# A fused decoder layer on one core: the SP queue's order and the interleaving of the other engines' steps are rewritten

## The chip, the core and the metric

The kernel runs on one core of one Trainium2 chip. The core has five engines that work side by side and meet only at semaphores: TensorE (PE in the profile: matrix products; PEld is its weight load), VectorE (DVE), ScalarE (ACT), GpSimd (POOL) and SyncE (SP, which here only issues DMA transfers). Each engine takes its instructions strictly in the order in which they are written. The metric is the device time of one execution in microseconds (us); of several runs the median counts.

## The reference

A decoder layer is applied to x of shape (32, 100, 256), 32 sequences of 100 tokens, with a context ctx of shape (32, 361, 256):

```
x = layernorm(x + self_attention(x))            # 16 local heads and 4 latent heads, mixed by a gate, then out_w
x = layernorm(x + cross_attention(x, ctx, ctx)) # 16 heads; q and k are normalised per head
x = layernorm(x + switch_ffn(x))                # 8 experts, 200 places each; a token without a place stays as it is
```

In the self-attention a gate mixes the two kinds of heads: `gate * local + (1 - gate) * remote`. In the cross-attention the scores are `layernorm(q Wq) @ layernorm(k Wk)` per head, then a softmax over the 361 context tokens.

## The kernel before

The sequences pass through one software pipeline. Each iteration `it` works on several sequences at once, one per stage: A (products of the self-attention) on sequence n+2, B (its gate, out projection, norm and the cross queries) and K (cross keys) on n+1, X (row maxima of the cross scores) and V (cross values) on n, Y (cross scores, exponentials, products with V) on n-1, T (norm, router, placing in the experts' buffers) on n-2. Steps of a stage are numbered: A1, A2, K12, K34, B1 to B7, T2 to T6, V5, V6, Y1, Y2. The loop has 36 iterations; in 28 of them every stage has work. Behind it the eight experts run one after the other; the change leaves them alone.

Each engine has a function `body(it)` that lists its steps in the order in which it does them; nothing else sets the order. What each engine has in it:

- **PE** (`body`, L1059): A1 and A2 are the products of xT with the weights; they wait for xT. `cross_maximum(it, n)` (L991), n = 0 to 15, forms the scores of one head for the row maxima. They lie in two buffers of PSUM (MX), so number n can start only when DVE has read number n-2. Number 0, called X0 here, also waits until the stacked keys (Kst) and queries (Qst) have landed. `self_maxima` (L853 to L865) does the same for the self-attention, `cross_scores` (L1009) and `self_scores` (L886, L891) form the scores for the exponentials. K12(it, t) (L825, L826 with cT) is half t of the key projection, K34 (L971) its mean square. B3 transposes `mixed`, B6 is the query projection, B7 (L960) its mean square from `sqq`, X1 (L997) transposes the maxima, Y1 and A6 are the products with the values, Y2 and A7 transpose their results back.
- The small products share two PSUM banks, MI0 and MI1. The list `MISC` gives the order of their use: its entries take the two banks in turn, and a step can start only when the step two entries before it has been read out (`enter`).
- **DVE**: copies A1 and A2 out into QK, takes the 16 `cross_max` (L1445) and two `self_max`, T3 (sum and statistics), `norm2`, B2, `gate_sum`, `gating` (it ends with `gated`), B4, `norm1`, `key_norm`, `key_low`, `route_to`, `place_in`, `queries`, Y2, A7.
- **ACT**: the exponentials `cross_exp` (L1207) and `self_exp` (L1197), copies out of PSUM (among them OxU, which empties Y1's bank), K12 and K34, `rstd`, `gate_exp`, `high_k`, `high_q`, B6 (qc, then sqq), B7.
- **POOL**: `pair_sums`, `self_lo`, `gate_local`, `gate_remote`, `mix` (it makes `mixed` from `gated`), `keep_x2`, `x1_bias`, `query_low`, `scatter`.
- **SP**: loads cT (L535), xT (L543) and xn (L551) for later sequences. QK, the keys and the queries are each written to DRAM (`bounce_...`, L564 and L586) and read back in another layout (`stack_...`, L574, L578, L597): the stack waits until the write has landed. `load_c` for n+2 waits until V6 of sequence n has read the old cT; `load_x` for n+3 until A2 of n+1 has read the old xT; `bounce_keys` waits for `key_low`, `bounce_queries` for `query_low`.

Of the kernel before, what the change touches and what calls it, by code (L numbers as in the profile page):

```python
# [59 lines left out]
MISC = ["A1", "A2", "T2", "K1", "B1", "T3", "B2", "K2", "K3", "T4", "B3", "K4", "B4", "A4", "T5", "V5", "T6",  # L60
        "B5", "B6", "X1", "B7", "Y1", "V6", "A6", "Y2", "A7"]
# [98 lines left out]
def decoder_kernel(nc, io):  # L160
    ctx = ExitStack()
    with ctx:
# [360 lines left out]
        def _(sp):  # L523
# [152 lines left out]
        def _(pool):  # L676
# [84 lines left out]
            def body(it):  # L761
# [32 lines left out]
        def _(pe):  # L794
# [266 lines left out]
            def body(it):  # L1061
# [8 lines left out]
                if x: cross_maximum(it, 2); cross_maximum(it, 3); cross_maximum(it, 4)  # L1070
                if b: B1(it)
                if t: T3(it)
                if y: cross_scores(it, 3)
                if x: cross_maximum(it, 5)
                if b: B2(it)
                if x: cross_maximum(it, 6)
                if y: cross_scores(it, 4)
                if k: K12(it, 1)
                if x: cross_maximum(it, 7); cross_maximum(it, 8); cross_maximum(it, 9)
                if k: K34(it, 0)  # L1080
# [9 lines left out]
                if y: cross_scores(it, 6)  # L1090
                if a: self_maxima(it, 1)
                if y: cross_scores(it, 7)
                if a: A4(it)
                if t: T5(it)
                if x: cross_maximum(it, 13)
                if v: V56(it, [0, 1])
                if t: T6(it)
                if x: cross_maximum(it, 14)
                if a: self_scores(it, 0)
# [676 lines left out]
```

## Time and profile before

| | |
|---|---|
| median of 3 runs | 1540.39 us (1537.62 to 1549.59) |
| profiled execution | 1558.85 us, of which the trace spans 1557.0 |
| PE busy | 1211.0 us, 78% of the span, 11098 matmuls |
| PEld, DVE, ACT, POOL busy | 881.9, 842.6, 673.5, 335.7 us |
| mean granted TensorE clock | 0.903 of full speed |
| DMA | 134.99 MB, 87 GB/s over the span |

PE is the busiest engine, and what matters is when it stands still in its main loop and for whom. A row of the timeline gives the start (us from the span's start), the duration, the engine, the line of the kernel, the operation, out<-in by the program's names, the shape, how many instructions the row merges and, in brackets, the idle time ahead of it and what ended it. SPq is SP's queue: its rows are DMA issues, not transfers. A share of busy time is an average over stages with different limits, so the argument goes by single iterations.

### The profile page before, as it was taken

The numbers are of one execution on the slowest core, as the hardware profiler recorded it, in microseconds if no ns is written. First come the engines' busy times: TensorE is split into PE (matmuls) and PEld (weight loads), VectorE is DVE, ScalarE is ACT, GpSimd is POOL, SyncE is SP. The second block draws the span as 40 slices with busy tenths as digits, with TensorE's granted clock in tenths as the row PEclk, the third lists the DMA queues.
The fourth block names the chain that finished last, engine by engine and source line by source line (L and its number), as shares of the span: only waits on it lengthen the run. The fifth ranks groups of instructions, "written<-read, shape, count | busy, mean of one in ns | idle before, by whom it ended". The sixth has DMA issues, their size and how long they took to land.

```text
span 1557.0 us, 33961 instructions
## 1 busy us (share of the span) xinstructions
PE 1211.0 (78%) x11098; PEld 881.9 (57%) x11098; DVE 842.6 (54%) x2482; ACT 673.5 (43%) x1611; POOL 335.7 (22%) x485
## 2 busy tenths in 40 slices
PE   3577777888778888888887888788878887675885
PEld 2355555555555555666555566565555565454774
DVE  4234456566665656565556665666566655433432
ACT  0123445444454445444545454555455545432110
POOL 2111112122222222222222222222212222100111
PEclk9667989899999989889999999999999989866998
DMA  4233332233333333333333333334333333106542
GB/s 152 50 78 70 83 85 62 64 86 86 75 84 84 84 84 84 84 84 82 85 78 86 78 77 81 87 74 91 76 84 84 84 83 76 45 10 211 194 148 72
DMA packets 187012, 134.99 MB, mean 87 GB/s; under 512 B 95798, under 2 KB 182762, under 8 KB 186734
## 3 DMA queue, kind: packets, MB, share of 16 engines
q1 hardware_dynamic: 181778, 127.50, 34.3%
q0 software_dynamic: 3200, 6.61, 1.4%
q8 instruction: 29, 0.48, 0.1%
q10 hardware_dynamic: 1984, 0.23, 0.1%
q14 instruction: 21, 0.17, 0.0%
HBM read 91.06 MB, written 43.00 MB: 86 GB/s over the span
## 4 chain that ended last, share of the span: by engine, by line
PE 32%; issue 15%; DVE 14%; DMA 9%; POOL 5%; ACT 4%; SPq 3%; DVEq 1%; POOLq 0%; ACTq 0%
PE MI L825 7%; PE MI L826 6%; DMA xT<-in_xT 5%; PE MI L1022 4%; PE MX L1138 4%; DVE negmax_x L1445 3%; DVE negmax_s L1438 2%; DVE Khl L1520 2%; PE ST L825 2%; PE ST L826 1%; DMA self_stack<-self_halves 1%; ACT QKhl L1214 1%; PE MX L853 1%; PE MI L971 1%; SPq L535 1%
## 5 line engine op out<-in xcount | busy, mean ns | idle before, releaser
L1445 DVE TENSOR_REDUCE negmax_x<-MX 100x1 bf16<-100x361 f32 x512 | 261.6, 529 | 108.9 <-PE MX L991 107.9
L1207 ACT ACTIVATE wide<-ST 128x800 f32<-128x800 f32 (+1 forms) x256 | 169.9, 665 | 345.8 <-PE ST L1009 345.0
L991 PE MATMUL MX<-stacked,Qst 96*128 96x361 f16 x512 | 154.8, 331 | 119.0 <-DVE negmax_x L1445 67.1
L991 PEld LDWEIGHTS MX<-stacked,Qst 96*128 96x128 f16 x512 | 53.0, 106 | 201.0 <-DVE negmax_x L1445 133.1
L825 PE MATMUL MI<-xT,weights 128*128 128x100 f32 (+1 forms) x320 | 78.0, 333 | 49.2 <-DMA xT<-in_xT 48.3
L719 POOL TENSOR_TENSOR QKhl<-QK,QKhl 128x900 f16<-128x900 f32 x32 | 60.5, 1890 | 256.2 <-ACT QKhl L1214 256.2
L1009 PE MATMUL ST<-Qst,stacked 112*128 112x200 f16 x768 | 112.1, 257 | 0.3 <-ACT wide L1207 0.3
L1416 DVE TENSOR_SCALAR QK<-MI,small,parity_s 128x100 f32<-128x100 f32 x128 | 42.6, 374 | 103.4 <-PE MI L826 99.4
L734 POOL TENSOR_TENSOR x_all<-x,bpv 100x256 f32 (+1 forms) x32 | 23.2, 725 | 342.5 <-DVE x L1496 342.5
L825 PEld LDWEIGHTS MI<-xT,weights 128*128 128x128 f32 (+1 forms) x320 | 56.7, 224 | 69.7 <-DMA xT<-in_xT 40.0
L1009 PEld LDWEIGHTS ST<-Qst,stacked 112*128 112x128 f16 x768 | 70.7, 102 | 29.2 <-issue 10.1
L725 POOL TENSOR_TENSOR Qhl<-Qx,Qhl 128x400 f16<-128x400 f32 x32 | 30.2, 945 | 235.6 <-ACT Qhl L1279 235.6
L1022 PE MATMUL MI<-wide,Vx 128*32 128x100 f32 (+1 forms) x3072 | 78.3, 260 | 0.0
L1022 PEld LDWEIGHTS MI<-wide,Vx 128*32 128x32 f32 (+1 forms) x3072 | 70.9, 115 | 7.5 <-issue 7.4
L826 PE MATMUL MI<-xT,weights 128*128 128x100 f32 (+1 forms) x320 | 74.2, 322 | 0.0
L853 PE MATMUL MX<-mask_q,identb 100*128 100x400 bf16 (+1 forms) x128 | 46.3, 453 | 30.0 <-DMA self_stack<-self_halves 26.2
L1438 DVE TENSOR_REDUCE negmax_s<-MX 100x8 bf16<-100x800 f32 x64 | 63.0, 984 | 4.2 <-PE MX L859 4.2
L1197 ACT ACTIVATE Ps<-ST 100x800 f32<-100x800 f32 x64 | 53.4, 834 | 24.7 <-PE ST L891 24.7
L825 PE MATMUL MI<-weights,cT 128*128 128x256 f32 (+1 forms) x192 | 63.7, 414 | 0.5 <-issue 0.5
L1502 DVE TENSOR_TENSOR qn<-qc,rsq 128x200 f32<-128x200 f32 x32 | 11.8, 368 | 92.6 <-ACT rsq L1266 92.6
L971 PE MATMUL MI<-early,small 128*128 128x361 f32 x128 | 60.1, 555 | 1.1
L826 PEld LDWEIGHTS MI<-xT,weights 128*128 128x128 f32 (+1 forms) x320 | 59.4, 229 | 0.0
(259 smaller groups left out, 2889.7 us busy)
## 6 DMA issues: line engine op xcount, KB each, us to landing
stacked<-key_halves SPq DMA_DIRECT2D x96, 180.5 KB, 4.7
self_halves<-QKhl SPq DMA_DIRECT2D x32, 450.0 KB, 2.9
cT<-in_cT SPq DMA_DIRECT2D x32, 361.0 KB, 3.7
key_halves<-Khl SPq DMA_DIRECT2D x32, 361.0 KB, 2.8
self_stack<-self_halves SPq DMA_DIRECT2D x64, 150.0 KB, 3.9
Qst<-query_halves SPq DMA_DIRECT2D x96, 100.0 KB, 4.3
early<-in_w SPq DMA_DIRECT2D x8, 1024.0 KB
self_stack<-self_halves SPq DMA_DIRECT2D x32, 225.0 KB, 3.7
```

Of the source, the lines that this page charges most:

```text
L719: pool.tensor_tensor(QKhl[:, LOW], QK[:].rearrange("p t n -> p (t n)"), QKhl[:, HIGH], ALU.subtract).then_inc(a_lo, 1)
L825: pe.matmul(out, lhs(0), rhs(0), start=True, stop=False)
L826: return pe.matmul(out, lhs(1), rhs(1), start=False, stop=True)
L853: pe.matmul(MX[:, i, 0:n], identb[0:S], mask_q[:, 0:n], start=True, stop=True)
L971: pe.matmul(ps[:, 0:M], average[:], sqk[:, t], start=True, stop=True).then_inc(filled[step], 1)
L991: pe.matmul(MX[:, n % 2, 0:M], Qst[p][0:96, n * S:n * S + 128], Kst[p][0:96, n // 2 * M:(n // 2 + 1) * M], start=True, stop=True).then_inc ...
L1009: mm = pe.matmul(ST[:, first + i, c:c + 2 * S], Kst[p][:, k:k + 128], Qst[p][:, 2 * pair * S:2 * (pair + 1) * S], start=True, stop=True)
L1022: mm = pe.matmul(ps[VW * j:VW * (j + 1), g * S:(g + 1) * S], Vx[p][0:n, kt, 4 * g + j], Px[0:n, c:c + S], start=(kt == 0), stop=(kt == 2))
L1138: mm = pe.matmul(MX[0:S, s, 0:D], hT[:, m, s * S:(s + 1) * S], W2[p][:, m], start=(m == 0), stop=(m == 7))
L1207: act.activation(cross_part(Px, u), ST[0:n, first:first + 2, 0:width], ACT.Exp).then_inc(st_exp, 1)
L1438: dve.tensor_reduce(out[:, 2 * g:2 * g + 2], MX[0:S, :, 0:400].rearrange("p i (u k) -> p i u k", k=S), X, ALU.max, negate=True).then_inc(m ...
L1445: dve.tensor_reduce(negmax_x[:, n:n + 1], MX[0:S, n % 2, 0:M], X, ALU.max, negate=True).then_inc(max_read, 1)
```

## The change

Only the order of steps changes; no instruction is added or taken away apart from the register moves that go with waits. SP's `body` is written anew:

```diff
             def body(it):
+                if it.n + 3 < B:
+                    load_x(Seq(it.n + 3, it.j))
+                if it.n + 2 < B:
+                    load_n(Seq(it.n + 2, it.j))
                 if it.has("A"):
                     bounce_self(it)
                     stack_self(it)
                 if it.has("K"):
                     bounce_keys(it)
-                if it.n + 2 < B:
-                    load_c(Seq(it.n + 2, it.j))
-                if it.n + 3 < B:
-                    load_x(Seq(it.n + 3, it.j))
+                    stack_keys(it)
                 if it.has("B"):
                     bounce_queries(it)
                 if it.n + 2 < B:
-                    load_n(Seq(it.n + 2, it.j))
-                if it.has("K"):
-                    stack_keys(it)
+                    load_c(Seq(it.n + 2, it.j))
                 if it.has("B"):
                     stack_queries(it)
```

So xT and xn are loaded at the head of the round, the keys' stack stands directly behind the keys' write, and cT is loaded between the queries' write and their stack. On POOL `mix` moves ahead of `keep_x2`, and `x1_bias` behind `query_low`:

```diff
-                if b: gate_local(Bs, it); gate_remote(Bs, it)
+                if b: gate_local(Bs, it); gate_remote(Bs, it); mix(Bs)
                 if t: keep_x2(T)
-                if b: mix(Bs); x1_bias(Bs); query_low(it)
+                if b: query_low(it); x1_bias(Bs)
                 if t: scatter(T)
```

On PE, DVE and ACT many steps change places, and `MISC` follows PE's new order. The parts of which the prediction speaks, PE's first, then ACT's, then DVE's:

```diff
+                if k: K12(it, 0)
                 if x: cross_maximum(it, 0); cross_maximum(it, 1)
-                if k: K12(it, 0)
...
+                if k: K34(it, 0); K12(it, 1)
                 if x: cross_maximum(it, 10)
+                if b: B3(it)
                 if y: cross_scores(it, 5)
                 if x: cross_maximum(it, 11)
+                if y: cross_scores(it, 6)
                 if t: T4(it)
                 if x: cross_maximum(it, 12)
-                if b: B3(it)
...
                 if b: B6(it)
-                if x: cross_maximum(it, 15); X1(it)
                 if a: self_scores(it, 2)
+                if x: X1(it)
                 if b: B7(it)
...
+                if a: self_exp(it, 1)
                 if b: B6(it)
                 if x: X1(it)
-                if a: self_exp(it, 1)
-                if b: B7(it)
+                if a: self_exp(it, 2)
+                if b: B7(it); high_q(it)
                 if y: copy_out("Y1", it, OxU[:], lambda ps: ps[:, 0:4 * S], (filled["Y2"], it.of("Y").done(back=1)))
-                if a: self_exp(it, 2)
-                if b: high_q(it)
...
                 if x: cross_max(it, 5)
+                if b: B2(it)
+                if x: cross_max(it, 6); cross_max(it, 7)
                 if t: T3(it)
-                if b: B2(it)
-                if x: cross_max(it, 6)
```

The new text is one line shorter by line 793, so PE's lines are one less after the change (L991 is L990).

PE, from the last products of A2 (MI<-rkvh,pairsum) to the first maxima of the cross scores (L991) before:

```order
L826 MATMUL MI<-rkvh,pairsum 50x64
L1009 MATMUL ST<-Qst,stacked 128x200 x4
L935 MATMUL MI<-small,Ox 128x100 x2
L1009 MATMUL ST<-Qst,stacked 128x200 x2
L991 MATMUL MX<-stacked,Qst 128x361 x2
L825 MATMUL MI<-cT,WkC 128x361
L826 MATMUL MI<-cT,WkC 128x361
```

The same place after the change:

```order
L825 MATMUL MI<-rkvh,pairsum 50x64
L1008 MATMUL ST<-Qst,stacked 128x200 x4
L934 MATMUL MI<-small,Ox 128x100 x2
L1008 MATMUL ST<-Qst,stacked 128x200 x2
L824 MATMUL MI<-cT,WkC 128x361
L825 MATMUL MI<-cT,WkC 128x361
L990 MATMUL MX<-stacked,Qst 128x361 x2
```

K12(it, 0) (MI<-cT,WkC) moved from behind the first two maxima to ahead of them.

PE, from K34(it, 0) (L971, MI<-early,small) to `self_maxima(it, 0)` (L853) before; MI<-small,mixed is B3 and MI<-small,x2w is T4:

```order
L971 MATMUL MI<-early,small 128x361
L991 MATMUL MX<-stacked,Qst 128x361
L1009 MATMUL ST<-Qst,stacked 128x200 x2
L991 MATMUL MX<-stacked,Qst 128x361
L935 MATMUL MI<-small,x2w 128x100 x2
L991 MATMUL MX<-stacked,Qst 128x361
L935 MATMUL MI<-small,mixed 128x100 x2
L971 MATMUL MI<-early,small 128x361
L853 MATMUL MX<-mask_q,identb 128x500 x2
```

The same place after the change:

```order
L970 MATMUL MI<-early,small 128x361
L824 MATMUL MI<-cT,WkC 128x361
L825 MATMUL MI<-cT,WkC 128x361
L990 MATMUL MX<-stacked,Qst 128x361
L934 MATMUL MI<-small,mixed 128x100 x2
L1008 MATMUL ST<-Qst,stacked 128x200 x2
L990 MATMUL MX<-stacked,Qst 128x361
L1008 MATMUL ST<-Qst,stacked 128x200 x4
L934 MATMUL MI<-small,x2w 128x100 x2
L990 MATMUL MX<-stacked,Qst 128x361
L970 MATMUL MI<-early,small 128x361
L852 MATMUL MX<-mask_q,identb 128x500 x2
```

B3 moved from behind the last of the thirteen maxima to directly behind the eleventh.

ACT, from the copy of x1T (B5) to the end of the iteration before; Ps and Pl are `self_exp`, qc and sqq B6, lnq and rsq B7, OxU the copy of Y1, Qhl `high_q`:

```order
L1163 ACTIVATE x1T<-MI 128x200
L1273 ACTIVATE Khl<-early,small 128x361
L1197 ACTIVATE Ps<-ST 100x800
L1254 ACTIVATE qc<-MI,bqC 128x100 x2
L1258 ACTIVATE sqq<-MI,bqC 128x100 x2
L1231 ACTIVATE turned_x<-MI 16x100
L1233 DMA Qst<-turned_x 1x16x100
L1197 ACTIVATE Ps<-ST 100x800
L1264 ACTIVATE lnq<-MI,eps 128x200
L1266 ACTIVATE rsq<-lnq 128x200
L1163 ACTIVATE OxU<-MI 128x400
L1197 ACTIVATE Pl<-ST 50x400
```

The same place after the change:

```order
L1197 ACTIVATE Ps<-ST 100x800
L1254 ACTIVATE qc<-MI,bqC 128x100 x2
L1258 ACTIVATE sqq<-MI,bqC 128x100 x2
L1231 ACTIVATE turned_x<-MI 16x100
L1233 DMA Qst<-turned_x 1x16x100
L1197 ACTIVATE Pl<-ST 50x400
L1264 ACTIVATE lnq<-MI,eps 128x200
L1266 ACTIVATE rsq<-lnq 128x200
L1279 ACTIVATE Qhl<-Qx 128x400
L1163 ACTIVATE OxU<-MI 128x400
```

The second `self_exp` now stands ahead of B6, the third ahead of B7, and the copy to OxU behind `high_q`.

## Rows read from the trace of the kernel before

**Rows 1.** Windows: stretch, its us, each engine's busy us (instructions), granted clock, DMA
```profile
436.95:1279.80 842.85, 689.08 (x6909) 493.33 (x6910) 510.85 (x1491) 421.91 (x1008) 204.85 (x295) 0.95 0.37 82
...
801.91:840.75 38.84, 31.04 (x329) 22.21 (x330) 24.34 (x71) 20.06 (x48) 9.75 (x14) 1.00 0.37 83
840.75:880.79 40.04, 32.16 (x329) 23.07 (x329) 24.34 (x71) 20.17 (x48) 9.75 (x14) 0.96 0.37 81
```

**Rows 2.** Waits of PE: for what, total us, times, longest us
```profile
PE MI L825 <- DMA xT<-in_xT: 48.3, 29, 4.3
PE MX L991 <- DMA Qst<-query_halves: 45.9, 21, 7.0
```

**Rows 3.** Timeline of SP's queue, one iteration: issue's start us, duration us, transfer
```profile
831.76 0.36 SPq L586 DMA_DIRECT2D key_halves<-Khl  x1
836.77 0.62 SPq L535 DMA_DIRECT2D cT<-in_cT  x1
837.68 0.59 SPq L543 DMA_DIRECT2D xT<-in_xT  x1
838.51 0.41 SPq L586 DMA_DIRECT2D query_halves<-Qhl  x1
...
841.91 1.87 SPq L597 DMA_DIRECT2D Qst<-query_halves  x3
```

**Rows 4.** Timeline of PE, the same iteration and the next one's start
```profile
808.44 0.47 PE L991 MATMUL MX<-stacked,Qst 96*128 96x361 f16 x2 [1.90 <-DMA Qst<-query_halves]
808.78 0.85 PE L825 MATMUL MI<-cT,WkC 128*128 128x361 f32 x2
...
810.07 0.51 PE L1009 MATMUL ST<-Qst,stacked 112*128 112x200 f16 x4
...
819.82 0.34 PE L935 MATMUL MI<-small,mixed 100*128 100x100 f32 x2
...
821.19 0.59 PE L853 MATMUL MX<-mask_q,identb 100*128 100x500 bf16 x2
...
832.20 0.22 PE L997 MATMUL MI<-identb,negmax_x 100*128 100x100 bf16 x1 [0.97 <-DVE negmax_x L1445]
...
832.74 0.53 PE L960 MATMUL MI<-sqq,small 128*128 128x200 f32 x2
...
836.49 0.89 PE L905 MATMUL MI<-Ps,Vs 100*32 100x100 f32 x32
...
840.75 0.47 PE L825 MATMUL MI<-xT,weights 128*128 128x100 f32 x2 [1.39 <-DMA xT<-in_xT]
...
847.60 0.47 PE L991 MATMUL MX<-stacked,Qst 96*128 96x361 f16 x2 [2.22 <-DMA Qst<-query_halves]
```

**Rows 5.** Timeline of DVE, the same iteration
```profile
806.83 0.25 DVE L1429 TENSOR_SCALAR QK<-MI,small 64x50 f32<-64x50 f32 x1
808.88 0.98 DVE L1445 TENSOR_REDUCE negmax_x<-MX 100x1 bf16<-100x361 f32 x2 [1.80 <-PE MX L991]
810.77 1.49 DVE L1445 TENSOR_REDUCE negmax_x<-MX 100x1 bf16<-100x361 f32 x3 [0.92 <-PE MX L991]
...
818.28 0.42 DVE L1477 TENSOR_TENSOR gated<-differ,gate 100x256 f32<-100x256 f32 x1
```

**Rows 6.** Timeline of POOL, the same iteration
```profile
818.87 0.72 POOL L730 TENSOR_TENSOR mixed<-gated,rem 100x256 f32<-100x256 f32 x1 [1.02 <-DVE gated L1477]
...
837.01 0.95 POOL L725 TENSOR_TENSOR Qhl<-Qx,Qhl 128x400 f16<-128x400 f32 x1 [7.22 <-ACT Qhl L1279]
```

**Rows 7.** Timeline of ACT, the same iteration
```profile
831.58 0.58 ACT L1258 ACTIVATE sqq<-MI,bqC 128x100 f32<-128x100 f32 x2
...
833.47 0.84 ACT L1197 ACTIVATE Ps<-ST 100x800 f32<-100x800 f32 x1 [0.69 <-PE ST L891]
...
835.55 0.51 ACT L1163 ACTIVATE OxU<-MI 128x400 f32<-128x400 f32 x1 [0.51 <-PE MI L1022]
...
836.33 0.53 ACT L1279 ACTIVATE Qhl<-Qx 128x400 f16<-128x400 f32 x1
```

More of the change, by code:

```diff
@@ L1089, in body @@
                 if b: B4(it)
-                if y: cross_scores(it, 6)
+                if y: cross_scores(it, 7)
                 if a: self_maxima(it, 1)
-                if y: cross_scores(it, 7)
+                if t: T5(it)
                 if a: A4(it)
-                if t: T5(it)
                 if x: cross_maximum(it, 13)
                 if v: V56(it, [0, 1])
+                if x: cross_maximum(it, 14)
+                if b: B5(it)
+                if a: self_scores(it, 0)
+                if x: cross_maximum(it, 15)
                 if t: T6(it)
-                if x: cross_maximum(it, 14)
-                if a: self_scores(it, 0)
-                if b: B5(it)
                 if a: self_scores(it, 1)
                 if b: B6(it)
-                if x: cross_maximum(it, 15); X1(it)
                 if a: self_scores(it, 2)
+                if x: X1(it)
                 if b: B7(it)
@@ L1291, in body @@
                 a, k, b, x, y, t, v = (it.has(stage) for stage in "AKBXYTV")
-                if y: cross_exp(it, 0)
+                if y: cross_exp(it, 0); cross_exp(it, 1)
+                if a: self_hi(it)
                 if t: copy_out("T2", it, OxT[:], halves)
-                if y: cross_exp(it, 1)
-                if a: self_hi(it)
                 if k: K12(it, 0)
+                if b: copy_out("B1", it, latT[:], lambda ps: ps[0:64, 0:S])
                 if y: cross_exp(it, 2)
-                if b: copy_out("B1", it, latT[:], lambda ps: ps[0:64, 0:S])
+                if t: rstd(it.of("T"), rs2, ln2, mv2, t_ln, t_rs)
                 if y: cross_exp(it, 3)
-                if t: rstd(it.of("T"), rs2, ln2, mv2, t_ln, t_rs)
+                if b: gate_exp(it)
                 if y: cross_exp(it, 4)
-                if k: K12(it, 1)
-                if b: gate_exp(it)
-                if k: K34(it, 0)
-                if y: cross_exp(it, 5)
+                if k: K34(it, 0); K12(it, 1)
+                if b: copy_out("B3", it, mixT[:], halves)
+                if y: cross_exp(it, 5); cross_exp(it, 6)
                 if t: copy_out("T4", it, x2T[:], halves)
-                if b: copy_out("B3", it, mixT[:], halves)
-                if k: high_k(it, 0); K34(it, 1)
-                if y: cross_exp(it, 6)
+                if k: K34(it, 1)
+                if y: cross_exp(it, 7)
                 if a: A4(it)
+                if b: rstd(it.of("B"), rs1, ln1, mv1, b_ln, b_rs)
+                if k: high_k(it, 0)
                 if t: router_exp(it)
-                if y: cross_exp(it, 7)
-                if b: rstd(it.of("B"), rs1, ln1, mv1, b_ln, b_rs)
                 if v: values(it, [0, 1])
                 if b: copy_out("B5", it, x1T[:], halves)
+                if a: self_exp(it, 0)
                 if k: high_k(it, 1)
-                if a: self_exp(it, 0)
+                if a: self_exp(it, 1)
                 if b: B6(it)
                 if x: X1(it)
-                if a: self_exp(it, 1)
-                if b: B7(it)
+                if a: self_exp(it, 2)
+                if b: B7(it); high_q(it)
                 if y: copy_out("Y1", it, OxU[:], lambda ps: ps[:, 0:4 * S], (filled["Y2"], it.of("Y").done(back=1)))
-                if a: self_exp(it, 2)
-                if b: high_q(it)
                 if v: values(it, [2])
@@ L1611, in body @@
                 if a: self_max(it, 1)
+                if t: route_to(it)
+                if b: norm1(it)
+                if x: cross_max(it, 13); cross_max(it, 14)
                 if k: key_norm(it, 1)
[L1613 to L1616 removed]
+                if x: cross_max(it, 15)
+                if k: key_low(it, 0); key_low(it, 1)
                 if t: place_in(it)
[L1618 to L1620 removed]
                 if b: queries(it)
```

33 lines of the change are left out of this document (12 added, 21 removed).

## The prediction

> **What bounds the kernel now.** The main loop comes first. Between 436.95 and 1279.80 us, 21 iterations take 842.85 us, 40.14 each; one that keeps the full TensorE clock takes 38.84, with PE busy for 31.04 of it [rows 1]. 24.34 of DVE, 20.06 of ACT and 9.75 of POOL lie inside the same stretch [rows 1], so PE is the engine that the others must not make wait. Next, who it waits for. Over the whole run it waits 48.3 us at A1, the first product of an iteration, until xT has landed, 29 times (1.67 each), and 45.9 us at X0 (`cross_maximum(it, 0)`) until Qst has landed, 21 times [rows 2].
>
> The reason for the first stands in SP's queue, which works strictly in order. It writes the keys at 831.76 and then stands at `load_c` until V6, the last reader of the old cT, is done; cT goes out at 836.77, xT behind it at 837.68, the queries' write at 838.51, and the queries' stack only at 841.91 [rows 3]. A1 then starts at 840.75 after 1.39 of waiting and X0 at 847.60 after 2.22 [rows 4].
>
> **The path of one iteration** closes over three legs [rows 1, 4]:
> - leg I, A1 to X0: 801.91 to 808.44, 6.53;
> - leg II, X0 to the first matmul of `self_maxima(it, 0)` (L853): 808.44 to 821.19, 12.75;
> - leg III, from there to the next A1: 821.19 to 840.75, 19.56.
>
> The three make 38.84. I work out what the change does to each.
>
> **Leg I: 6.5, no gain.** K12(0) now stands ahead of X0. It needs the MI bank that A2 filled, and that is free when the last QK write ends: 806.83 + 0.25 = 807.08 [rows 5], 5.2 after A1. K12(0) itself takes 808.78 to 810.07, 1.29 [rows 4]. So X0 comes 5.2 + 1.3 = 6.5 after A1. Qst could in principle let X0 start earlier, but PE is not there earlier. If the bank were free at once, up to 1.3 less; I take 0.
>
> **Is Qst there by then?** `query_low` ends at 837.01 + 0.95 = 837.96 [rows 6]. SP is then free, because `stack_keys` has its own place behind the keys' write: that write took until 834.9 at most (831.76 plus about 3.4, what the queries' write of 838.51 to 841.91 took [rows 3]), and with three issues taking 1.87 as for Qst [rows 3] the keys' stack is out near 836.8. The queries' write goes at 838.0 and not 838.51. To its stack it is 3.40, from the stack to X0 another 5.69 (841.91 to 847.60) [rows 3, 4]: X0 could start at 847.1, or 25.9 after `self_maxima`, with B7 as late as now. B7 comes 0.2 earlier (leg III): 25.7. Today three keys' transfers lie just ahead of the queries' stack and after the change one cT does, so I take 0.5 off as an estimate: 25.2. PE would be at X0 after the new leg III (18.6) plus 6.5, at 25.1. X0 waits 0.1 to 0.6; I take 0.15.
>
> Here a rule speaks against the change. The Trainium skill, "DMA: Bandwidth & Descriptors", section "Queues, rings and completion order", says that SP owns one row of rings and that each DMA engine takes descriptors in ring order. By it the cT that now goes out between the queries' write and their stack stands ahead of the stack, and nothing may be taken off: X0 waits 0.6 and the sum below turns from -0.25 to +0.2 an iteration. The row of the queries' write (3.40 with cT and xT ahead of it) neither shows nor excludes that; it is the third rival.
>
> **Leg II: 12.75 to 13.35, +0.6.** DVE is the pace here, and what counts are the holes in its row of maxima.
> - The hole of 0.92 that K12(0) makes between the second and third maximum [rows 5] goes: -0.92.
> - B3, the transpose of `mixed`, stood behind the last of these maxima; now it stands right behind the eleventh, on an engine that works in order, ahead of the twelfth. `mixed` ends at 818.87 + 0.72 = 819.59 [rows 6], 0.89 after its input `gated` (818.28 + 0.42 = 818.70 [rows 5]). Then come B3's 0.34 [rows 4] and 0.44 from a maximum's matmul to its reduce (808.44 to 808.88 [rows 4, 5]): 1.67 without a new maximum, less the 0.5 that the eleventh takes (0.98 for two [rows 5]): +1.15. PE meanwhile stands idle for longer, since the eleventh matmul needs only the ninth reduce: about 2.5.
> - DVE now takes B2's sum right behind the sixth maximum, while PE has to do the seventh first: a hole between 0 and the 0.92 that K12(0) makes; I take +0.4.
>
> Sum: +0.6, with ends of -0.9 (nothing lost) and +1.2 (both holes at their largest). T3's place and Y6's only exchange neighbours; the self-attention's stack needs nothing earlier than now, because PE gets to it no earlier.
>
> **Leg III: 19.56 to 18.55, -1.0.**
> - xT is loaded at the start of the SP round, an iteration ahead: -1.39 [rows 4].
> - X1's wait of 0.97 for the last maximum [rows 4] goes, because that maximum stands two steps earlier. But B7 follows X1, and it needs `sqq` from ACT. That ends now at 831.58 + 0.58 = 832.16, 0.58 before B7 (832.74) [rows 4, 7]. ACT's new order puts `self_exp(it, 1)`, 0.84 [rows 7], and one `high_k` ahead of it and takes the last `cross_exp` away. Of the 0.97 at most all and at least nothing is left; I take -0.2.
> - A6 needs the bank that Y1 filled, so it needs ACT's copy to OxU. That copy ends at 836.06 now, 0.43 before A6 (836.49) [rows 4, 7]. In the new order it stands behind `high_q`, which starts at 836.33 and waits for DVE [rows 7]: 836.33 + 0.43 to the next ACT step + 0.51 = 837.3, 0.8 after A6. With B7 0.2 earlier: +0.6 (ends 0 and 0.8).
>
> POOL's moved steps (`mix` ahead of `keep_x2`, `query_low` ahead of `x1_bias`) cost nothing: 29 us of each iteration it is idle [rows 1], and the next reader of `x1_bias` is an iteration away. Without that cover each would cost its 0.72 or so [rows 6].
>
> **The sum** is 0 + 0.6 - 1.0 + 0.15 = -0.25 an iteration, times the 28 in which every stage runs: -7. The waits for xT above 1.39 (48.3 - 29 x 1.39 = 8 us [rows 2, 4]) I count by half: -4. Together -11 on the profiled execution's own 1558.85 (span 1557.0 and 1.85 around it): 1548. That execution was 18.5 above the median of the runs, 1540.39, so in runs it is 1529; I say **1528**.
>
> **The clock** is the term I cannot sum. An iteration with the granted clock at 0.96 takes 40.04 against 38.84 at 1.00 [rows 1]: 1.20 for a short fall to the lower of the two levels (1.2 and 2.4 GHz). The mean iteration loses 1.30 that way [rows 1]. The change closes the idle time at the iteration's start and opens a longer one at B3. In the forecast these cancel.
>
> **Rivals.**
> 1. *The gain is large.* Falls of the clock go with the waits at A1 and X0. All iterations at full clock and 38.84 - 0.25 = 38.6: 28 x (38.6 - 40.14) = -43, and 4 for the long waits: 1540 - 47 = 1493. For it: A1's and X0's waits, 3.6 together in one iteration [rows 4], are the largest pair. Against it: B3's. Chance 0.23.
> 2. *Slower: B3 costs clock.* An idle PE of 2.5 in one piece exceeds each of today's (2.22 at X0 [rows 4]). If each iteration falls once more, it is 1.20 - 0.25 = +0.95, 28 x 0.95 = +27: 1567. It decides from a fall more in two of three iterations (0.67 x 1.20 - 0.25 = 0.55, 28 x 0.55 = 15.4, one per cent). The Trainium skill, "TensorE: Matmul & The Clock Gate", Part 1, says that the lower clock is the default and activity lifts it; that is this rival's mechanism. The rows bear it out in part only: the iteration from 801.91 has all of today's waits and keeps 1.00 [rows 1]. Chance 0.22.
> 3. *The change buys nothing, since Qst is the bound.* X0 waits for as long as A1 gained: +0.2 an iteration and long waits that only move: 28 x 0.2 = +6, 1546; with leg III's gain whole, 1535. I put it at 1542. Chance 0.13.
>
> **Chances and range.** The forecast has 0.42 and its own range of 1512 to 1545 (legs II and III at half of their ends). A measurement of this kernel can tell about one per cent, 15.4 us, from no change. Faster by more than that (below 1525): rival 1 and 0.17 of the forecast, 0.40. Within one per cent: 0.24 of the forecast and 0.12 of rival 3, 0.36. Slower: rival 2 and 0.02 left, 0.24. The range leaves out a tenth on each side: from rival 1's 1493 to 1562, five below rival 2.
>
> **What would show it.** Right: no wait for xT at A1; K12(0) ahead of X0 waiting for QK; a PE idle of 2 to 3 before B3 for `mixed`; X1 without a wait, B7 waiting for `sqq`, A6 for OxU; an iteration of 38.4 to 38.7 at full clock. Wrong: leg II at 12 or less (B3's wait hidden), X0 waiting over 1 for Qst (rival 3), the granted clock in the loop above 0.98 (rival 1) or below 0.93 (rival 2, today 0.95 [rows 1]).

## The result and the profile after

The changed kernel takes **1501.26 us** (median of 4 runs, 1497.61 to 1504.92); the kernel before took 1544.61 beside it (4 runs). The ratio is 0.972, with a 95% interval of 0.967 to 0.978: faster by 2.8%. The prediction was 1528, with a range of 1493 to 1562. The time lies in the range but below the forecast's own 1512 to 1545: the sign was right, and the gain was 43 where the sum had 11. That it lies in the range is in part luck: the range's lower end, 1493, was set for rival 1, whose mechanism did not occur.

Windows of the changed kernel: iterations five to ten of the loop, the 21 behind them that answer to the first of [rows 1], and one at full clock (stretch, its us, busy us and instructions of PE, PEld, DVE, ACT and POOL, granted clock, DMA):

```profile
178.80:410.60 231.80, 196.44 (x1977) 140.56 (x1975) 143.38 (x426) 116.79 (x288) 57.80 (x83) 0.95 0.36 86
410.60:1231.00 820.40, 686.32 (x6910) 493.09 (x6909) 503.87 (x1491) 409.63 (x1008) 204.66 (x295) 0.95 0.36 84
488.00:525.96 37.96, 30.95 (x331) 22.43 (x330) 24.03 (x71) 19.44 (x48) 9.81 (x15) 1.00 0.38 88
```

Iterations five to ten of the kernel before:

```profile
185.80:436.90 251.10, 201.89 (x1974) 144.81 (x1974) 146.20 (x426) 121.11 (x288) 58.52 (x84) 0.92 0.35 79
```

The span fell from 1557.0 to 1503.1, by 53.9; the profiled execution before was a long one, so this is more than the 43 between the medians. Of the 53.9, 19.3 lie in these six iterations (251.10 to 231.80), 10 in the four ahead of them (162.1 to 152.2, from A1 to A1 in the timeline), 22.5 in the 21 steady ones (842.85 to 820.40, which is 40.14 to 39.07 each) and 2 in the rest. An iteration at full clock went from 38.84 [rows 1] to 37.96. The mean clock of the steady stretch is 0.95 before and after.

Waits of PE after (for what, total us, times, longest us), to set against [rows 2]:

```profile
PE MI L934 <- POOL mixed L729: 55.9, 30, 3.6
...
PE MI L959 <- ACT sqq L1258: 22.2, 31, 1.0
...
PE MI L824 <- DVE QK L1426: 16.7, 28, 0.6
...
PE MI L904 <- ACT OxU L1163: 10.5, 28, 0.4
```

The two waits of [rows 2], for xT and for Qst, are gone (Qst keeps 6.9 us in two waits at the start), and four waits that the prediction named stand in their place. PE's timeline of the iteration from 488.00 shows their places:

```profile
493.22 0.88 PE L824 MATMUL MI<-cT,WkC 128*128 128x361 f32 x2 [0.60 <-DVE QK L1426]
...
494.54 0.47 PE L990 MATMUL MX<-stacked,Qst 96*128 96x361 f16 x2
...
505.68 0.36 PE L934 MATMUL MI<-small,mixed 100*128 100x100 f32 x2 [2.69 <-POOL mixed L729]
...
507.75 0.59 PE L852 MATMUL MX<-mask_q,identb 100*128 100x500 bf16 x2
...
518.89 0.61 PE L959 MATMUL MI<-sqq,small 128*128 128x200 f32 x2 [0.68 <-ACT sqq L1258]
...
523.15 0.89 PE L904 MATMUL MI<-Ps,Vs 100*32 100x100 f32 x32 [0.41 <-ACT OxU L1163]
```

DVE's timeline of the same iteration has three holes ahead of or between its maxima: before B2's sum, before T3's and before the twelfth maximum, behind B3.

```profile
498.38 0.42 DVE L1458 TENSOR_TENSOR rem<-MI,biases 100x256 f32<-100x256 f32 x1 [0.58 <-PE MI L929]
...
500.64 0.42 DVE L1533 TENSOR_TENSOR res<-MI,x_all 100x256 f32<-100x256 f32 x1 [0.96 <-PE MI L825]
...
506.41 1.21 DVE L1442 TENSOR_REDUCE negmax_x<-MX 100x1 bf16<-100x361 f32 x2 [1.23 <-PE MX L990]
```

Leg I is 488.00 to 494.54, 6.54; leg II 494.54 to 507.75, 13.21; leg III 507.75 to 525.96, 18.21. SP's queue at the end of that iteration (issues, as in [rows 3]):

```profile
520.55 1.87 SPq L597 DMA_DIRECT2D stacked<-key_halves  x3
523.61 0.36 SPq L586 DMA_DIRECT2D query_halves<-Qhl  x1
524.22 0.62 SPq L535 DMA_DIRECT2D cT<-in_cT  x1
526.38 1.88 SPq L597 DMA_DIRECT2D Qst<-query_halves  x3
```

From the queries' write to their stack it is 2.8 and no longer 3.4 [rows 3]. The list of DMA issues has the median time from the issue of a Qst transfer to its landing; the kernel before, then after (KB each, median us):

```profile
Qst<-query_halves SPq DMA_DIRECT2D x96, 100.0 KB, 4.3
```

```profile
Qst<-query_halves SPq DMA_DIRECT2D x96, 100.0 KB, 2.8
```

### The profile page after: what moved, and what is told of

The parts are those of the page before. It is cut to its first block, busy times and chain, and to the rows that moved or that the text cites. A ratio compares the mean times of both kernels' runs of the same rounds, so it can differ in the third digit from the quotient of the medians.

```text
span 1503.1 us, 33998 instructions
## 1 busy us (share of the span) xinstructions
PE 1197.1 (80%) x11098; PEld 869.5 (58%) x11098; DVE 831.8 (55%) x2482; ACT 654.4 (44%) x1611; POOL 335.3 (22%) x485
## 4 chain that ended last, share of the span: by engine, by line
PE 35%; issue 24%; DVE 16%; ACT 12%; POOL 6%; DMA 3%; ACTq 3%; SPq 1%; DVEq 1%; POOLq 0%
PE MI L824 5%; PE MI L825 4%; PE MX L1138 4%; DVE negmax_x L1442 3%; DVE negmax_s L1435 3%; PE MX L990 2%; ACT Ps L1197 2%; PE MI L934 2%; PE MI L913 2%; PE MI L1029 2%; PE MI L904 2%; PE ST L824 2%; PE ST L1008 2%; PE ST L825 2%; POOL mixed L729 1%
## 5 line engine op out<-in xcount | busy, mean ns | idle before, releaser
L1207 ACT ACTIVATE wide<-ST 128x800 f32<-128x800 f32 (+1 forms) x256 | 163.4, 665 | 214.6 <-PE ST L1008 214.6
L990 PE MATMUL MX<-stacked,Qst 96*128 96x361 f16 x512 | 170.2, 343 | 48.1 <-DVE negmax_x L1442 32.3
L990 PEld LDWEIGHTS MX<-stacked,Qst 96*128 96x128 f16 x512 | 51.2, 100 | 125.3 <-DVE negmax_x L1442 87.2
L1008 PE MATMUL ST<-Qst,stacked 112*128 112x200 f16 x768 | 117.5, 266 | 2.5 <-ACT wide L1207 2.5
L1186 ACT ACTIVATE stat<-stat,eps 100x1 f32<-100x1 f32 x32 | 9.4, 294 | 159.1 <-DVE stat L1540 159.1
L824 PE MATMUL MI<-cT,WkC 128*128 128x361 f32 x128 | 59.6, 551 | 19.4 <-DVE QK L1426 16.7
L824 PE MATMUL MI<-xT,weights 128*128 128x100 f32 (+1 forms) x320 | 68.2, 297 | 0.9 <-DVE bpv L1398 0.9
L825 PE MATMUL MI<-xT,weights 128*128 128x100 f32 (+1 forms) x320 | 64.4, 285 | 0.0
L1524 DVE RECIPROCAL recip_x<-MI 100x16 f32<-100x16 f32 x32 | 8.2, 258 | 100.1 <-PE MI L1029 100.1
L852 PE MATMUL MX<-mask_q,identb 100*128 100x400 bf16 (+1 forms) x128 | 40.7, 404 | 28.3 <-DMA self_stack<-self_halves 20.0
L824 PE MATMUL MI<-weights,cT 128*128 128x256 f32 (+1 forms) x192 | 60.8, 398 | 0.0
L825 PE MATMUL MI<-weights,cT 128*128 128x256 f32 (+1 forms) x192 | 58.0, 384 | 0.0
L824 PEld LDWEIGHTS MI<-xT,weights 128*128 128x128 f32 (+1 forms) x320 | 48.5, 193 | 15.2 <-issue 13.4
## 6 DMA issues: line engine op xcount, KB each, us to landing
stacked<-key_halves SPq DMA_DIRECT2D x96, 180.5 KB
```

The costliest lines, as they stand in the source:

```text
L824: pe.matmul(out, lhs(0), rhs(0), start=True, stop=False)
L825: return pe.matmul(out, lhs(1), rhs(1), start=False, stop=True)
L990: pe.matmul(MX[:, n % 2, 0:M], Qst[p][0:96, n * S:n * S + 128], Kst[p][0:96, n // 2 * M:(n // 2 + 1) * M], start=True, stop=True).then_inc ...
L1008: mm = pe.matmul(ST[:, first + i, c:c + 2 * S], Kst[p][:, k:k + 128], Qst[p][:, 2 * pair * S:2 * (pair + 1) * S], start=True, stop=True)
L1207: act.activation(cross_part(Px, u), ST[0:n, first:first + 2, 0:width], ACT.Exp).then_inc(st_exp, 1)
```

## Experiments

What was open: whether the gain is SP's or the interleaving's; what the new waits cost; and why the clock falls. Each batch had the kernel before on the same chip (medians of 1542 to 1546), so a difference of a few us between kernels of two batches says little. The legs given below are means over the 21 steady iterations, if not said otherwise.

### SP's order alone, and the interleaving alone

The first is the kernel before with the new SP `body`, the second the changed kernel with the old one.

> The kernel before with the new SP queue alone; PE, ACT, DVE and POOL keep the old order. Theory A (the queue brings the gain, the new interleaving costs some of it back): A1 waits for nothing, so leg III is 19.56 - 1.39 = 18.2; X0 stands 4.6 after A1 on PE and finds Qst a little late (5.3 after A1); self_maxima is then bound by the self-attention's stack, 18.1 to 18.4 after A1. 36.5 an iteration at full clock against 37.96 after the change, so about 1465 us, faster than the whole change. Rival B (the new interleaving is needed for the new queue to pay): X0's wait grows by what A1's shrinks, only A1's long waits at the start go, 1505 to 1530 us.

> The changed kernel with the old SP queue: the new interleaving alone. Theory A: xT arrives behind V6 as before, leg III is 19.3, leg I 6.5, leg II 13.2: 39.0 an iteration at full clock, 1545 to 1560 us, no gain. Rival B (half the gain is the interleaving's): 1515 to 1530 us.

SP's order alone took 1468.3 (ratio 0.950, 0.943 to 0.958): faster than the whole change. The new interleaving alone took 1536.4 (0.996, 0.992 to 0.999). The first is what theory A had, the second lies between the theories. So SP's order is worth 75 us, and the interleaving that was to go with it takes 33 of them back. In the first, an iteration takes 37.53, and the two without a fall of the clock 36.62 and 36.68; X0 starts 5.75 after A1 and still waits about 1.1 there for Qst (45.3 us over the whole run). In the second, PE has the new waits and also 32.9 us of the old one for xT.

### Which part of SP's order

One kernel moves only the loads of xT and xn to the head, the other only the keys' stack behind the keys' write. The first:

```diff
+                if it.n + 3 < B:
+                    load_x(Seq(it.n + 3, it.j))
+                if it.n + 2 < B:
+                    load_n(Seq(it.n + 2, it.j))
                 if it.has("A"):
                     bounce_self(it)
...
-                if it.n + 3 < B:
-                    load_x(Seq(it.n + 3, it.j))
                 if it.has("B"):
                     bounce_queries(it)
-                if it.n + 2 < B:
-                    load_n(Seq(it.n + 2, it.j))
```

> The kernel before with only load_x and load_n moved to the head of SP's round; load_c stays ahead of the queries' write and the keys' stack just ahead of the queries' stack. Theory A (the two waits of PE lie in one loop that closes through the queries' write: what A1 no longer waits, X0 waits longer): 1530 to 1542. Theory B (each wait is a cost of its own): 1.39 in each of 28 iterations and the long waits, 1490 to 1503.

The second:

```diff
                 if it.has("K"):
                     bounce_keys(it)
+                    stack_keys(it)
                 if it.n + 2 < B:
                     load_c(Seq(it.n + 2, it.j))
...
-                if it.has("K"):
-                    stack_keys(it)
                 if it.has("B"):
                     stack_queries(it)
```

> The kernel before with only the keys' stack moved to directly behind the keys' write; cT and xT keep their places behind the wait for V6. Theory A (the keys' stack just ahead of the queries' stack is what delays Qst; its transfers landed 4.3 us after their issue before the change and 2.8 after it): X0's wait of 2.2 falls to 0.7, xT is late as before, 1495 to 1510. Theory B (Qst lands early for another reason, cT's and xT's transfers being away from it): 1530 to 1542. Theory C (the gain of the SP body needs both parts, since whatever one wait loses the other takes): 1525 to 1542 here and with xT alone, though both together gave 1468.

xT first took 1540.5 (0.994, 0.990 to 0.998), as theory A had it; its profiled execution, from which the waits are read, took 1547.3. Keys' stack first took 1587.0 (1.029, 1.021 to 1.037), **slower**, which no theory expected. Waits of PE, xT first:

```profile
PE MX L991 <- DMA Qst<-query_halves: 90.2, 31, 7.5
```

and keys' stack first:

```profile
PE MI L824 <- DMA xT<-in_xT: 72.7, 30, 3.8
...
PE MX L852 <- DMA self_stack<-self_halves: 30.6, 18, 14.4
...
PE MX L990 <- DMA Qst<-query_halves: 13.4, 4, 7.7
```

The two waits of [rows 2], 48.3 and 45.9, are two ends of one loop. With xT early, its 48.3 vanish and Qst's grow by 44.3. With the stack early, Qst's fall by 32.5 and xT's grow by 24.4, 0.8 each. xT's transfer now has the keys' stack ahead of it: SP issues it 6.1 after the keys' write where it did 5.9, and it lands 3.8 after its issue where it took 3.2 before (medians), which together is that 0.8. The steady iteration was 40.77, and its clock 0.93; how much of the loss is the transfer's and how much the clock's these runs don't separate.

The third part of the order, cT behind the queries' write, was undone in the version of the next heading:

```diff
-                if it.has("B"):
-                    bounce_queries(it)
                 if it.n + 2 < B:
                     load_c(Seq(it.n + 2, it.j))
+                if it.has("B"):
+                    bounce_queries(it)
```

> The version with the SP body and K12(it, 0) ahead of X0 (1460 us when measured), and with cT loaded ahead of the queries' write instead of behind it; nothing else. With it only this move of the SP body is undone: xT stays at the head and the keys' stack behind their write. Theory A (the keys' stack and xT are what counts; V6 is done before query_low): 1457 to 1466. Theory B (cT ahead of the write delays the write's landing by 0.4 to 0.7 us, and so Qst, but X0 stands behind K12(0) and Qst has 0.7 us to spare): 1457 to 1470. Theory C (SP stands at load_c for V6 and the queries' write with it, so that X0 waits again for Qst, 1 us or more): 1485 or more.

It took 1474.3 (0.956, 0.950 to 0.961), between theories B and C, 14 more than with cT behind (1459.9, 0.937 to 0.951: the intervals just touch). The steady iteration is the same (37.55 against 37.54); in the profiled executions 7.5 us are lost in the first ten, where X0 waits again for Qst, up to 1.9, and the rest of the 14 is not placed. The write lands 3.9 after its issue with cT ahead of it and 2.8 without, and the stack behind it lands in 2.6 without cT ahead and in 3.0 with it (medians). So two moves were needed together, xT's and the keys' stack: each alone only passes the time on, and with both (and K12(0) ahead), but without cT's move, most of the gain is there. cT's place is worth the 14 at most.

### K12(0) ahead of X0

> The kernel before with the new SP body, and on PE K12(it, 0) ahead of X0 and X1 instead of behind them; nothing else. With the SP body alone 1468 us was measured and X0 waited 1.0 to 1.4 us for Qst in each iteration. Theory A (K12(0) fills a wait that is there anyway, and the hole of 0.92 us that it made in DVE's row of maxima goes): 0.9 less in each of 28 iterations, about 1443. Theory B (the hole comes back at another place of leg II, since the maxima wait for T3, B2 or the twelfth matmul in any case): 1460 to 1470. Theory C (K12(0) has to wait for QK, so X0 comes later than Qst lands): 1470 to 1480.

PE's part:

```diff
+                if k: K12(it, 0)
                 if x: cross_maximum(it, 0); cross_maximum(it, 1)
-                if k: K12(it, 0)
```

It took 1459.9 (0.944, 0.937 to 0.951) against 1468.3 (0.950, 0.943 to 0.958), a difference that the intervals don't separate. The time is theory B's, the mechanism is not: the hole does not come back in leg II. Leg I went from 5.75 to 6.54, leg II from 13.22 to 11.94, and leg III from 18.56 to 19.07, so that the mean iteration is the same (37.53 and 37.54). Over the iterations at full clock alone (two against four) leg I grows by 0.63, leg II falls by 0.89 and leg III grows by 0.06. So the 0.92 hole goes, as the prediction had it, and X0, which could have started at 5.8 but now stands behind K12(0)'s wait for QK (theory C's mechanism), pays for most of it.

### The copy to OxU behind high_q

Taken out of the change (ACT):

```diff
-                if b: B7(it); high_q(it)
+                if b: B7(it)
                 if y: copy_out("Y1", it, OxU[:], ...
+                if b: high_q(it)
```

> The changed kernel with the copy to OxU back ahead of high_q on ACT. Theory A: A6's wait of 0.41 goes, the queries come 0.5 later, but Qst has 1.4 to spare at X0: 0.4 an iteration, about 1490 us. Rival: the next step (the copy of A6 to OsT, or the queries) takes the wait over, 1500 us.

And put alone into the version with SP's order:

> The kernel before with the new SP body, and on ACT the copy to OxU behind the last self_exp and high_q, as the change has it; nothing else. With the SP body alone 1468 us was measured. Theory A (A6 waits for OxU, 0.4 us or more in each iteration, and the clock falls more often, whatever the interleaving of the rest): 1480 to 1500, as taking this swap out of the whole change gave 30 back. Theory B (the copy's late place costs only beside the change's other moves): 1465 to 1473.

Taken out of the change: 1471.4 (0.953, 0.946 to 0.960), 30 less, where the path's wait alone would have given 11; both theories had less gain. Put in alone: 1480.8 (0.956, 0.948 to 0.964), in theory A's range and 13 more than without, which the intervals don't separate; A6 waits up to 0.8 there (21.7 us in all), of which X0's wait for Qst gives a part back, and the mean clock of the steady stretch is 0.95 where it was 0.96. Windows of the change without it, the steady stretch and one iteration:

```profile
405.80:1199.20 793.40, 652.97 (x6912) 473.53 (x6910) 502.42 (x1491) 410.37 (x1008) 204.44 (x295) 0.99 0.38 87
...
557.30:594.80 37.50, 30.89 (x331) 22.41 (x329) 23.95 (x71) 19.53 (x48) 9.80 (x15) 1.00 0.38 89
```

At full clock 37.50 against 37.96: 0.46, A6's wait. But the mean iteration went from 39.07 to 37.78, by 1.29, since 18 of 21 iterations now keep the full clock, where 3 did. So 0.46 is the path's and 0.8 the clock's. This holds in the change's interleaving; with SP's order alone the same swap changed the clock by 0.01.

### B3 and the interleaving of leg II

First B3 alone was put back behind X12, with its copy on ACT and MISC:

```diff
                 if x: cross_maximum(it, 10)
-                if b: B3(it)
...
                 if x: cross_maximum(it, 12)
+                if b: B3(it)
                 if k: K34(it, 1)
```

> The changed kernel with B3 moved back behind the thirteenth maximum on PE (and its copy behind x2T's on ACT, the MI list to match). Theory A: PE's wait of 2.7 for mixed goes, leg II falls from 13.2 to about 12.1; the self-attention's stack, 18.1 after A1, leaves room for that (self_maxima stands at 19.75): 1.1 an iteration, about 1470 us. Rival C (B3's wait is hidden, because the next maxima are bound by DVE or by the stack anyway): 1495 to 1505 us. Rival D (the wait also lowers the clock): under 1460 us, with the granted clock in the loop above that of the changed kernel.

It took 1528.4 (0.989, 0.981 to 0.996): 27 **more** than the change, against all theories. PE's timeline in that kernel:

```profile
519.01 0.39 PE L934 MATMUL MI<-small,mixed 100*128 100x100 f32 x2 [0.73 <-ACT early L1171]
...
520.36 0.87 PE L970 MATMUL MI<-early,small 128*128 128x361 f32 x2 [0.95 <-ACT x2T L1163]
```

The wait for `mixed` is gone, but in the new neighbourhood B3 waits for ACT to empty K12(1)'s bank and K34(1) for it to empty T4's, each two entries before in `MISC` and now only just filled. Leg II is 14.67, where the change has 13.82. That run prices a bad order of banks, not B3. So the whole stretch from X2 to B4 was put back to the order of before on PE, ACT and DVE, in the change with the early copy to OxU (PE's part; `MISC` follows):

```diff
                 if y: cross_scores(it, 2)
-                if x: cross_maximum(it, 2)
+                if x: cross_maximum(it, 2); cross_maximum(it, 3); cross_maximum(it, 4)
+                if b: B1(it)
+                if t: T3(it)
                 if y: cross_scores(it, 3)
-                if x: cross_maximum(it, 3)
-                if b: B1(it)
-                if x: cross_maximum(it, 4); cross_maximum(it, 5); cross_maximum(it, 6)
+                if x: cross_maximum(it, 5)
                 if b: B2(it)
-                if x: cross_maximum(it, 7); cross_maximum(it, 8)
-                if t: T3(it)
-                if x: cross_maximum(it, 9)
+                if x: cross_maximum(it, 6)
                 if y: cross_scores(it, 4)
-                if k: K34(it, 0); K12(it, 1)
+                if k: K12(it, 1)
+                if x: cross_maximum(it, 7); cross_maximum(it, 8); cross_maximum(it, 9)
+                if k: K34(it, 0)
                 if x: cross_maximum(it, 10)
-                if b: B3(it)
                 if y: cross_scores(it, 5)
                 if x: cross_maximum(it, 11)
-                if y: cross_scores(it, 6)
                 if t: T4(it)
                 if x: cross_maximum(it, 12)
+                if b: B3(it)
                 if k: K34(it, 1)
                 if a: self_maxima(it, 0)
                 if b: B4(it)
-                if y: cross_scores(it, 7)
+                if y: cross_scores(it, 6); cross_scores(it, 7)
```

> The change with the copy to OxU ahead of high_q (1471 us when measured), and with the interleaving of the kernel before from X2 to B4 on PE, ACT and DVE, MISC to match: T3 ahead of B2, K12(it, 1) behind Y4, T4 and B3 behind X11 and X12; K12(it, 0) stays ahead of X0. With the change's interleaving there PE waits 2.7 us for mixed in each iteration, which takes 37.6 us at full clock with a mean clock of 0.994. Theory A (B3's early place makes leg II longer by about 1.2, at no cost in clock): leg II at about 12, an iteration at 36.3 at full clock, clock unchanged: 1433 to 1445. Theory B (the work packed closer has the clock falls of the version with the SP body and K12(0) ahead, 0.957 in the loop): 1455 to 1470. Theory C (the waits for maxima take B3's place, leg II stays at 13): 1468 to 1475.

And B3 alone was moved forward in the version with SP's order and K12(0) ahead, where PE waits for neither of these two banks:

> The version with the SP body and K12(it, 0) ahead of X0 (1460 us when measured), and with B3 moved to directly behind X10, its copy on ACT ahead of cross_exp 5 and T4's, MISC to match; nothing else. Theory A (B3's early place costs what the prediction worked out): PE waits 2.5 us before B3 for mixed, leg II is 1.15 longer, 28 times is 32: 1485 to 1495. Theory B (the wait for mixed takes the place of waits for maxima that were there anyway): 1455 to 1468. Theory C (PE's wait of 2.5 in one piece costs a clock fall more in each iteration, 1.2 each): 1500 or more.

Leg II put back: **1416.8** (0.919, 0.914 to 0.924), 55 less than with the change's leg II, and 85 less than the change; that is theory A's mechanism, with more gain than it had. B3 forward alone: 1511.3 (0.981, 0.975 to 0.987), 51 more than without, which is theory C's range, though the wait for `mixed` is 1.7 there in each steady iteration and not 2.5. Windows of the first, the steady stretch and one iteration:

```profile
392.50:1146.90 754.40, 656.93 (x6910) 469.26 (x6909) 501.08 (x1491) 421.75 (x1008) 204.49 (x294) 1.00 0.39 91
464.30:500.10 35.80, 31.23 (x331) 22.30 (x330) 23.90 (x71) 20.09 (x48) 9.82 (x15) 1.00 0.39 91
```

and the steady stretch of the second, with its wait before B3:

```profile
410.50:1227.30 816.80, 699.49 (x6911) 496.34 (x6910) 512.78 (x1491) 424.56 (x1008) 205.14 (x295) 0.92 0.36 84
```

```profile
PE MI L934 <- POOL mixed L729: 54.5, 32, 3.6
```

At full clock leg II is 11.53 with the old order and 13.21 with the change's, everything else alike: 1.68, times 28 is 47 of the 55. B3 forward alone makes leg II longer by 0.93 (11.94 to 12.87), and the mean clock of the stretch falls from 0.96 to 0.92, so that the iteration grows by 1.36. The 0.93 is not the path's alone: in leg II itself the mean clock falls from 0.97 to 0.90.

### B7's wait for sqq

In the fastest version B6 was put ahead of the second `self_scores` on PE and of the second `self_exp` on ACT:

```diff
-                if a: self_scores(it, 1)
                 if b: B6(it)
-                if a: self_scores(it, 2)
+                if a: self_scores(it, 1); self_scores(it, 2)
```

> The version with the old leg II and the early copy to OxU (1417 us when measured), and with B6 ahead of self_scores 1 on PE and ahead of self_exp 1 on ACT, so that the second and third self_scores stand between B6 and B7; nothing else. In each iteration PE waits 0.68 us there for sqq before B7 (22.1 us in all), the wait that came in X1's place. Theory A (sqq is ready before B7, and nothing takes the wait's place): 0.6 less in each of 28 iterations, 1395 to 1405. Theory B (x1T or self_exp 1 is late instead, or A6 waits for the exponentials): 1412 to 1420. Theory C (PE packed closer loses clock, which stands at 0.998 in the loop now): 1420 or more.

It took 1413.5 (0.914, 0.908 to 0.921), as theory B had it; the intervals don't separate it from 1416.8. The wait of 0.68 is gone, and an iteration at full clock is shorter by 0.2 (35.58 against 35.80): leg III lost 0.55 and leg I grew by 0.35. The time moved to the next iteration's start. One iteration of this version at full clock:

```profile
532.70:568.30 35.60, 31.54 (x331) 22.40 (x330) 23.75 (x71) 20.27 (x48) 9.73 (x14) 1.00 0.40 91
```

## Why the prediction was right, and where it was not

**What bounds the kernel** was right, and can be put more sharply. The prediction treated A1's and X0's waits as two; the run with xT first showed one loop, in which 48.3 us of the one became 44.3 of the other.

**Leg I, 6.5**, measured 6.54. K12(0) waits 0.60 for QK at 5.2 after A1, as worked out.

**Qst**: the forecast had X0 wait 0.15, from transfers that it took to land 0.5 earlier than the 4.3 of before; no run shows that 0.5. They land 1.5 earlier (2.8), the last one 5.1 after A1 in the iteration from 488.00, with 1.4 to spare. This step failed in size: the keys' stack just ahead costs more than the estimate. Qst's transfers land in 4.3 before, in 3.8 when only xT and xn are moved, and in 2.7 when only the stack is; the stack costs xT behind it 0.6. In the steady iteration it moved nothing, since K12(0) holds X0 to 6.54. The rule that spoke against the change is that descriptors are taken in ring order (the Trainium skill, "DMA: Bandwidth & Descriptors", "Queues, rings and completion order"). The runs agree with it in sign: with cT ahead of it Qst's stack lands in 2.8 in the changed kernel and in 3.0 with K12(0) ahead, without cT in 2.6. That is 0.2 to 0.4, while the keys' stack that stood there before had cost 1.6 (4.3 to 2.7), and so X0 stayed unharmed.

**Leg II, 13.35 (+0.6)**, measured 13.21 (+0.46). K12(0)'s hole of 0.92 goes: the first six maxima follow one another in the changed kernel, and in the run with K12(0) ahead leg II lost 0.89 at full clock. B3's early place makes a hole of 1.23 where 1.15 was worked out, with PE idle for 2.69 where 2.5 was. B2's hole is 0.58 where 0.4 was taken; no run moves B2 alone. T3's hole is 0.96 where one of 0.86 stood before. The old order of the rest would have left 11.53 where 12.75 - 0.92 = 11.83 was expected, so together these moves cost 1.68 where 1.55 was taken. The sum leaves out that `key_norm`, 0.59 on DVE, now stands behind the thirteenth maximum and no longer ahead of it; no run moves it alone either.

**Leg III, 18.55 (-1.0)**, measured 18.21 (-1.35). X1 waits no longer, B7 waits 0.68 for `sqq` in its place (-0.29 where -0.2 was taken), and A6 waits 0.41 for OxU (+0.6 was taken, 0.46 came back when the copy was moved). xT's 1.39 is gone from A1.

**The sum**: an iteration at full clock takes 37.96 to 38.27 where 38.4 to 38.7 was named, -0.88 where -0.25 was forecast; the three legs' misses (0.15 for X0's wait, 0.14, 0.35) are all to the same side. That is 28 x 0.63 = 18 of the missing gain.

**The long waits, -4**: the term that failed most. Iterations one to ten gained 29 of the 53.9 us of span. The prediction counted there only xT's waits above 1.39, by half, and six of its 28 like iterations. In the kernel before, A1 of iteration six waits 4.3 for xT (its longest in [rows 2]) and that of the next one 3.2; after the change no wait for xT is left. These ten take 413 before, 400 with xT first, 423 with the stack first, 398 with the new interleaving alone, 385 with all of SP's order and 384 after. So SP's order is enough for nearly all of it, and the interleaving alone takes off 15 as well. Not all of the 29 need be the change's: the profiled execution of before was 14 longer than the median beside the change, that of after 4, and the mean clock of iterations five to ten is 0.92 in the one and 0.95 in the other.

**The clock cancels**: right for the steady stretch, 0.95 and 0.95, but by luck, since different falls cancelled. In the kernel before, the granted clock falls nine times in the 21 iterations within 1.4 us of an A1 and 14 times 17.6 to 20.5 behind it; after the change no fall is left near A1, but 10 begin 10.4 to 12.1 behind it and 8 begin 17.1 to 19.5 behind it. Over all runs, the versions in which the interleaving of leg III is the change's and OxU is copied early keep 0.99 and 1.00; the same with OxU late, or with the old leg III, have 0.92 to 0.97. Why is not shown.

**The rivals.** Rival 1 has the nearest time (1493), but not by its mechanism: the mean clock of the loop did not rise, and A1's and X0's waits went without it. The falls near A1 are gone with A1's wait, as it said, but others came. Rival 2 set B3's idle of 2.5 above each of today's; [rows 2] have longer ones, 4.3 and 7.0, but in the 21 steady iterations none over 2.4. It said that this idle would cost a fall in each iteration. In the changed kernel eight of the 18 falls begin in B3's idle or within 2 us behind it, as in the iteration from 679.67 (windows of B3's idle and of the fall):

```profile
694.60:697.60 3.00, 0.28 (x3) 0.05 (x1) 2.30 (x7) 2.37 (x7) 0.82 (x3) 1.00 0.68 102
...
699.20:702.40 3.20, 3.20 (x19) 1.95 (x18) 1.68 (x4) 1.59 (x4) 0.00 (x0) 0.50 0.00 0
```

In the change without the late copy B3's idle is as long, 2.7, and 18 of 21 iterations keep 1.00, so that an idle PE of this length is not enough. The same two places there, in the iteration from 557.30:

```profile
572.30:575.00 2.70, 0.03 (x1) 0.02 (x1) 2.06 (x7) 2.23 (x5) 0.86 (x3) 1.00 0.76 112
...
576.60:579.80 3.20, 2.85 (x24) 1.64 (x23) 2.45 (x6) 2.01 (x5) 0.00 (x0) 1.00 0.00 0
```

Yet B3 forward alone came with a lower clock, 0.92 for 0.96. The other ten falls of the changed kernel begin ahead of B3's idle. Windows of the iteration from 410.60, before its fall, in it and behind it:

```profile
417.10:422.40 5.30, 4.06 (x21) 2.02 (x20) 4.20 (x9) 2.07 (x5) 4.12 (x5) 1.00 0.23 87
422.80:425.80 3.00, 3.00 (x10) 1.84 (x9) 1.86 (x6) 0.89 (x3) 0.86 (x2) 0.50 0.71 143
426.40:448.80 22.40, 18.68 (x256) 14.23 (x254) 13.18 (x42) 14.08 (x37) 3.71 (x7) 1.00 0.27 59
```

The same stretch without the late copy, in which nothing falls:

```profile
563.80:569.20 5.40, 4.16 (x21) 2.05 (x20) 4.20 (x9) 2.12 (x5) 4.17 (x5) 1.00 0.23 85
```

PE does the same work in both just ahead of the fall (21 matmuls, 4.06 of 5.30 us and 4.16 of 5.40), to 1.2 GHz in one and not in the other. That activity lifts the clock (the Trainium skill, "TensorE: Matmul & The Clock Gate", Part 1) doesn't tell them apart. What the copy to OxU changes that makes the difference stays **open**, for both kinds of falls. Rival 3's mechanism, that X0 waits for what A1 gains, is exactly what xT first showed (0.994); it was the keys' stack that kept it from the whole change, and cT's place added 14 us at most.

**What was not seen**: that the interleaving, judged as a whole, is a loss. Its own terms summed to +1.03 (K12(0) -0.92, B3 +1.15, B2 +0.4, X1 -0.2, A6 +0.6), against -1.39 of xT, and stood in the working; it measured +1.3 on top of SP's order (36.65 to 37.96 at full clock). Part of it is a price that leg I hides: with SP's order alone X0 stands 5.75 after A1, and K12(0) ahead of it takes 0.8 of that back. The prediction added up both and didn't say that half of the change would do better alone.

## What to carry to other kernels

Two waits on transfers of one queue can be one loop: moving one transfer alone then gains nothing, or loses, and the order has to be changed as a whole. Price each part of a change by its own sum before adding them up: here the queue's order was worth 75 us, the step order took 33 back, and the best versions keep the first and only a part of the second. A step that is moved in a list that shares buffers in turn takes its neighbours' waits with it, so move it together with the order of the buffers and read the bank's waits, not only the operand's.

## What the runs showed of the hardware beyond the prediction

- Qst's transfers (100 KB each) land 4.3 us after their issue with the three of 180.5 KB of the keys' stack just ahead of them in SP's queue, and 2.7 when only that stack is moved away. With cT (361 KB) issued some 2.2 us ahead of them they land in 2.8 to 3.0, with cT 5.0 ahead in 2.6.
- In the change's interleaving one copy's place on ACT, worth 0.46 us of PE's time, moved the loop's mean granted clock from 0.95 to 0.99, worth 0.8 us more; with SP's order alone the same swap moved it from 0.96 to 0.95 only.
- The longest wait of PE in an iteration does not order the versions by clock: 2.7 us in every iteration with a mean of 0.99 (the change with OxU early), 1.2 us at most with 0.96 (SP's order and K12(0) ahead), 0.9 us at most with 1.00 (the old leg II).
- The fastest kernel of the study, 1413.5 us, has PE busy for 31.5 of 35.6 us in an iteration; what PE still waits for in its loop is mostly DVE.
